# Score masks of three-branch attention: mask products on the TensorE against index selections on the GpSimd

## The reference

```
def _attn(q, k, v, mask=None):
    s = jnp.einsum('bhqd,bhkd->bhqk', q, k) / np.float32(np.sqrt(HD))
    if mask is not None:
        s = jnp.where(mask, s, jnp.float32(-1000000000.0))
    return jnp.einsum('bhqk,bhkd->bhqd', jax.nn.softmax(s, -1), v)
causal = ii[:, None] >= ii[None, :]
o1 = _attn(q, k1, v1, causal[None, None])
o2 = _attn(q, ks, vs)                       # 128 selected keys, no mask
winmask = causal & (ii[:, None] - ii[None, :] < WINDOW)     # WINDOW = 32
o3 = _attn(q, kw, vw, winmask[None, None])
o = g[:, 0] * o1 + g[:, 1] * o2 + g[:, 2] * o3
```

## Time and profile before

| | |
|---|---|
| median of 3 runs | 1062.2 us (1062.18 to 1073.87) |
| profiled execution | 1067.6 us, span 1065.8 us |
| TensorE busy | 909.1 us, 85% |
| VectorE busy | 598.2 us, 56% |
| ScalarE busy | 432.7 us, 41% |
| GpSimd busy | 205.0 us, 19% |

### The profile page before, as it was taken

How to read it: one execution, slowest core, us unless ns; L and a number is a source line. 1 busy time by engine, 2 the same in 40 slices (tenths; PEclk the granted TensorE clock), 3 DMA queues, 4 the chain that set the end, 5 groups by cost and what they waited for, 6 DMA issues and landing times.

```text
span 1065.8 us, 21748 instructions
## 1 busy us (share of the span) xinstructions
PE 909.1 (85%) x8956; PEld 618.8 (58%) x8956; DVE 598.2 (56%) x1687; ACT 432.7 (41%) x724; POOL 205.0 (19%) x274
## 2 busy tenths in 40 slices
PE   3647689999998999989998999899989899888688
PEld 3426456566666666666666666666656565555356
DVE  5243454664587457745874587457755653633433
ACT  0001234452454255425542554255455444436631
POOL 1011100210124012311231123112312320131201
PEclk8658689999999999999999999999999999979855
DMA  7000000100000000000100010000100001200000
GB/s 184 1 1 5 1 6 2 42 21 26 21 21 21 26 21 22 21 26 10 32 21 26 9 33 22 21 6 27 31 21 22 21 26 36 54 21 22 1 4 18
DMA packets 27138, 25.28 MB, mean 24 GB/s; under 512 B 16480, under 2 KB 22240, under 8 KB 26912
## 3 DMA queue, kind: packets, MB, share of 16 engines
q1 hardware_dynamic: 27040, 23.90, 8.0%
HBM read 19.16 MB, written 4.72 MB: 22 GB/s over the span
## 4 chain that ended last, share of the span: by engine, by line
PE 62%; DVE 19%; ACT 8%; issue 6%; DMA 3%; POOL 2%; SPq 1%; DVEq 0%; POOLq 0%; ACTq 0%
PE ring L872 8%; PE side_a L606 5%; PE pv L911 4%; PE pv L893 4%; ACT pr L1114 3%; PE ring L827 3%; DVE rden L1588 3%; PE heads L815 3%; PE side_a L613 2%; PE heads L852 2%; DVE img L1306 2%; PE heads L812 2%; PE side_a L644 2%; PE ring L867 1%; PE ring L835 1%
## 5 line engine op out<-in xcount | busy, mean ns | idle before, releaser
L1114 ACT ACTIVATE pr<-ring 128x1024 f32<-128x1024 f32 (+1 forms) x128 | 120.7, 943 | 116.7 <-PE ring L876 66.1
L872 PE MATMUL ring<-kq 64*128 64x256 f32 (+2 forms) x1280 | 137.9, 343 | 0.8 <-ACT kq L1159 0.5
L872 PEld LDWEIGHTS ring<-kq 64*128 64x128 f32 x1280 | 93.2, 189 | 45.0 <-issue 35.8
L1151 ACT ACTIVATE kq<-ring 128x896 f32<-128x896 f32 x64 | 58.8, 919 | 93.9 <-PE ring L827 93.9
L1573 DVE TENSOR_REDUCE toks<-heads 128x2 f32<-128x512 f32 x64 | 44.2, 691 | 90.2 <-PE heads L857 89.1
L1598 DVE SCALAR_TENSOR_TENSOR ob<-pv,all_gates,scale 128x256 f32<-128x256 f32 x96 | 46.3, 483 | 75.0 <-issue 32.7
L1588 DVE RECIPROCAL rden<-pv 128x256 f32<-128x256 f32 x32 | 56.1, 1754 | 39.7 <-PE pv L893 39.7
L1578 DVE TENSOR_REDUCE toks<-heads 128x4 f32<-128x512 f32 x64 | 44.2, 690 | 53.4 <-PE heads L852 53.1
L606 PE MATMUL side_a<-img,wc_kv 128*128 128x256 f32 x208 | 58.5, 448 | 17.8 <-DVE keep L1309 16.3
L827 PE MATMUL ring<-early,toks 128*128 128x128 f32 x448 | 63.0, 282 | 11.5 <-ACT pr L1114 10.8
L1159 ACT ACTIVATE kq<-ring 128x256 f32<-128x256 f32 x64 | 24.4, 381 | 119.1 <-PE ring L835 119.1
(11 more groups left out here) (372 smaller groups left out, 1761.5 us busy)
## 6 DMA issues: line engine op xcount, KB each, us to landing
scale<-branch_scale SPq DMA_DIRECT2D x128, 96.0 KB, 2.3
branch_scale<-rden SPq DMA_DIRECT2D x32, 128.0 KB, 1.7
late<-in_late SPq DMA_DIRECT2D x1, 2158.5 KB, 8.6
xin<-in_x SPq DMA_DIRECT2D x16, 64.0 KB, 2.2
pr<-in_prep SPq DMA_DIRECT2D x1, 602.0 KB, 4.2
y<-ob SPq DMA_DIRECT2D x8, 64.0 KB, 1.9
kq<-in_masks SPq DMA_DIRECT2D x1, 480.0 KB, 8.6
toks<-in_final SPq DMA_DIRECT2D x1, 434.0 KB, 4.4
```

The source lines that it names most:

```text
L872: m = pe.matmul(ring[:, j, at:at + nq], kq[rows, k, key0:key0 + P], kq[rows, k, Q + q_:Q + q_ + nq], start=r % 2 == 0, stop=at > P)
L1114: act.activation(out, in_, ACT.Exp, scale=SCALE).then_inc(S("exp_done"), 1)
L1151: act.activation(kq[:, k, :], flat[:, 0:WIDE], ACT.Copy).then_inc(S("turned"), 1)
```

## The change

TensorE no longer multiplies masks into the scores; every score product starts and ends its own sum. GpSimd gets a function `scored`, run in part turned (behind the front's and back's slot late and ahead of weighed). It waits for `exp_done` of the step and then overwrites exponentials with zero where an index rule fails, by `affine_select` in place: one instruction of 2 x 128 elements in an even step; four in an odd step (512, 320, 256 and 320 elements), where the third waits for the first and the fourth for the second through the semaphore `later`. The last raises `masked`, and `denominators` waits for `masked` and no longer for `exp_done`.

```
+            def scored(t):
+                for n, r in each(scores_of, t):
+                    k = r // 2
+                    part = pr[:, k // 2 % 2, k % 2, 0:1024] if r % 2 == 0 else pr[:, k // 2 % 2, k % 2, 1024:1856]
+                    part = part.rearrange("p (j n) -> p j n", j=2)
+                    keys = 2 * P + BAND
+                    pool.wait_ge(S("exp_done"), n * PARTS + r + 1)
+                    if r % 2 == 0:
+                        nc.gpsimd.affine_select(part[:, :, 0:P], part[:, :, 0:P], [[0, 2], [1, P]], ALU.is_ge, 0.0, base=0,
+                                                channel_multiplier=-1).then_inc(S("masked"), 1)
+                        continue
+                    own, near = part[:, :, 0:2 * P].rearrange("p j (x n) -> p j x n", x=2), part[:, :, 2 * P:keys]
+                    nc.gpsimd.affine_select(own, own, [[0, 2], [0, 2], [1, P]], ALU.is_ge, 0.0, base=0,
+                                            channel_multiplier=-1).then_inc(S("later"), 1)
+                    nc.gpsimd.affine_select(near, near, [[0, 2], [1, BAND]], ALU.is_ge, 0.0, base=0,
+                                            channel_multiplier=-1).then_inc(S("later"), 1)
+                    pool.wait_ge(S("later"), n * PARTS + r)
+                    nc.gpsimd.affine_select(own[:, :, 1, :], own[:, :, 1, :], [[0, 2], [-1, P]], ALU.is_ge, 0.0,
+                                            base=WINDOW - 1, channel_multiplier=1)
+                    pool.wait_ge(S("later"), n * PARTS + r + 1)
+                    nc.gpsimd.affine_select(near, near, [[0, 2], [-1, BAND]], ALU.is_ge, 0.0, base=WINDOW - 1,
+                                            channel_multiplier=1).then_inc(S("masked"), 1)
...
             run("POOL", [front(n + 1) for n in range(B)], [back(n + 1, n) for n in range(B)],
-                weighed=weighed, filled=filled)
+                turned=scored, weighed=weighed, filled=filled)
...
                 else:
-                    for j in range(2):
-                        pe.matmul(ring[:, j, 0:2 * P + BAND], identb, score_b, start=True, stop=False)
                     pieces = [(0, K1 + P, P, P), (P, KW + P, P, P), (2 * P, KW, 0, BAND)]
...
-                                      kq[rows, k, Q + q_:Q + q_ + nq], start=r % 2 == 0, stop=at > P)
-                if r % 2 == 0:
-                    for j in range(2):
-                        m = pe.matmul(ring[:, j, 0:P], identb, score_b[:, 0:P], start=False, stop=True)
+                                      kq[rows, k, Q + q_:Q + q_ + nq], start=True, stop=True)
...
-                pe.wait_ge(S("exp_done"), of * PARTS + 4 * (g + 1))
+                pe.wait_ge(S("masked"), of * PARTS + 4 * (g + 1))
```

## The result

The changed kernel takes 1105.0 us (median of 4 runs, 1103.7 to 1106.5) against 1062.2 (4 runs, 1058.0 to 1073.9): 1.044 times as long, 95% interval 1.038 to 1.050. The forecast was 1072 in a range of 1044 to 1100. The profiled execution took 1104.0 us, with a span of 1102.3 against 1065.8; the two profiles thus differ by 36.5 us and the medians by 43.

A forecast was written before the change was run, and what follows sets the result against it. TensorE was taken to set the pace in most places. Removal -20, group 2 stall +17, last image +6, group 1 +3, VectorE beside GpSimd +6, closing gaps -2 give +10 on 1062.2: 1072 us, range 1044 to 1100.

The forecast's parts named there:

- The removal, -20 us: Mask products leaving TensorE's chain: gain 20 us, 25 at most, 15 if VectorE takes over more.
- The selections, 3.0 us a pair: GpSimd's price for a pair of heads, even plus odd step, midway between memset (2.0) and two-input rows (4.1).
- The stall of group 2, 17 us: TensorE waits at group 2's denominators for selections queued behind GpSimd's power: 2.8 us in each of images 1 to 6.
- 8 late: Last image: denominators start near 941 us, 8 us late behind the power; 6 us (4 to 8) taken as new.
- Group 1: Denominators of group 1 wait for the selections of step 7: 0.5 us kept, 6 times, 3 us (0 to 8).
- rival C: GpSimd behind the power decides and the clock falls: 1090 us, or 1102 with 2 us for each stall; chance 0.22.
- behind a stall those gaps close: TensorE idles 9% between 550 and 850 us; these gaps shrink behind a stall, so 2 us are taken off.
- VectorE beside GpSimd, 6 us: Some 80 SBUF-only VectorE instructions on the chain wait by chance for selections: 6 us (3 to 11).
- the two lines that I named: VectorE's L1306 and L1463, SBUF-only instructions: both were to have a higher mean.
- A: Cheap selections at the memset's price: 1057 us; chance 0.20.
- B: Stalls are absorbed and the removal's gain is whole, 25 us: 1037 us; chance 0.11.
- D: GpSimd becomes the bound, from 9 us for a pair's selections: 1150 us and more; chance 0.05.

The follow-up runs named there:

- held clock: Three kernels with useless TensorE products and the power in two halves: mask products 1051.9 us, no score masks 1033.7, selections on GpSimd 1050.8.
- the addition alone: Kernel before, mask products kept, plus GpSimd's selections with the denominators waiting for them: 1102.6 us, ratio 1.037.
- the removal alone: Kernel before without the mask products and with no selections, score masks left out altogether: 1054.0 us, ratio 0.988.
- the queue in another order: Changed kernel with selections of steps 10 and 11 earlier in GpSimd's queue and the power cut into two of 16 elements: 1076.1 us, ratio 1.013.
- the idle products: 22 and 40 unused TensorE products ahead of those waiting for `vtok` and `keep`; added to the changed kernel with reordered GpSimd queue: 1044.4 us, ratio 0.987.
- the short power: Changed kernel with the 32-element power on GpSimd replaced by a product of the same size, normalization left out: 1077.1 us, ratio 1.016.
- the change with idle products: Changed kernel, queue order unaltered, plus 22 and 40 unused TensorE products ahead of those waiting for `vtok` and `keep`: 1084.3 us, ratio 1.021.
- no masks and the divided power: Kernel before without score masks or selections, with unused TensorE products and the power in two halves: 1033.7 us, ratio 0.973.
- products and the divided power: Kernel before, mask products kept, with unused TensorE products and the power in two halves: 1051.9 us, ratio 0.988.

## Why the prediction was wrong

**The removal, -20 us.** At a held clock it is 17 us, so the working from the chain was sound. In the kernel alone it is 12 us, and beside the selections nothing. The gain has a condition that the working did not state: the clock must hold.

**The selections, 3.0 us a pair.** They cost 2.39. The middle between memset and two-input rows was too high, the stall depended little on it, and 346 us of GpSimd are under the forecast 400.

**The stall of group 2, 17 us.** It is where I put it, with GpSimd as its releaser: 2.31 us five times, in images 1 to 5, against 2.8 each six times; image 6 has none, and image 0, which I had left out, has 1.33. Together 13 us. With the measured selections the same sum gives 544.52 + 0.41 + 1.01 + 1.99 = 547.9, 2.1 us behind 545.8. The last image cost 7.4 us of waiting against 8 late, and the image took 84.1 us for 77.1 from its first to its last exponential, part of which is the variation of that place told above. Group 1, for which I had 3 us, waits 0.15 us at most.

**The clock, no term at all.** This is the step that failed. I gave the lower clock to rival C alone, at 2 us for each stall, and put it behind the stall. In the sum I took the opposite line: "behind a stall those gaps close", -2 us. In fact the change lengthens gaps at places where VectorE sets the time. The wait for `vtok` grows by the removal (0.93 us before and in the addition alone, 1.28 in the removal alone, 1.29 in the change), the one for `keep` by both parts (2.44 before, 2.90 in the removal alone, 2.71 in the addition alone, 3.19 in the change). Behind these two gaps the clock falls to its lower level, and that costs 4.2 us an image, some 21 us over images 1 to 5, of which the kernel before already lost 7.6 (540.9 against 533.3 us for five images of 106.65 us). The difference, 13.6 us, is the largest part of the 22.0 that the change costs in these images. Part of this hangs on the stall: without the stall and with the gaps as they are (the queue in another order) the idle products are worth 14.3 us in these images. That idle time of TensorE is needed for the loss is shown, since filling the two gaps ends it there. What decides in which image it comes is not: behind the same wait of 1.28 or 1.29 us interval 0 took 4.93 us with the short power, 4.93 or 6.49 in the removal alone, and 6.4 in the change. TensorE's busy time shows it: 30 to 40 us less was expected, 2 came. A row for it stood in the profile before: the convolution's 26 products in 7.59 us in image 3, behind a wait of 2.44, in a stretch whose clock of 0.99 I read as full.

**VectorE beside GpSimd, 6 us.** The term was of the right kind and too small. I spread it by chance over some 80 instructions, which gives 0.75 us an image. The selections' own cost, which holds this term, is 1.8 us an image, 0.7 of it in one place, where a moved instruction of GpSimd lands on VectorE's path each time. By the rule of the Trainium skill (SBUF — State Buffer, Who interferes with whom) a `tensor_scalar` of VectorE from SBUF to SBUF can enter a two-port mode and then excludes an instruction of GpSimd. The trace agrees with an exclusion: 1.70 us alone, 2.60 beside two additions of GpSimd; no row shows the mode. Of the two lines that I named, L1306 has a higher mean as forecast (436 to 565 ns), while L1463, now L1482, ran as before (median 292 ns, longest 696).

**Sum.** Over images 1 to 5 the change costs 22.0 us. The terms give 5 x (-2.52 + 1.83 + 2.38 + 4.24) = 29.6, less the 7.6 that the kernel before loses to its own clock: 22.0. Outside these images the profile shows 14.4 us more: 7.0 in the last image, where 7.4 us of waiting stand behind the power, 6.0 in the tail behind it, 1.4 elsewhere. These I did not take apart. In the tail the granted clock is 0.68 after and 0.73 before, but both places vary by as much between profiles (the last image by 7 us in one kernel). Of the rivals, C was nearest with 1102, by luck: its price of a selection, 4.1 us a pair, was not met (2.39), and its 12 us for the clock belong behind the stall, where the 48 products take 1.79 us in the change as before; only the addition alone and the change with idle products showed them at the lower clock. A and B are ruled out by the stall, D by 31% of GpSimd.

## What to carry to other kernels

Work taken from an engine is worth its time only if the engine then isn't sooner at a place where another sets the pace; in this kernel the time came back as idle time of TensorE, and with it the clock fell and took the rest of the gain. So before a product is removed, look in the timeline for each wait behind it and for whether the same group of products behind it takes longer in one image than in another. In an engine that works in order, put a new step ahead of the longest instruction of its neighbourhood, and check on whose path the steps land that it pushes back.

## What the runs showed that I had not expected

Products without any use make the kernel faster. 62 of them an image take 2.6 us of TensorE, and with the new order of the queue images 1 to 5 take 531.0 us with them against 545.4 without.

The last 35 us run at a mean granted clock of 0.50 or 0.79 in each of the fifteen profiles. The kernel before and the change have 0.50 there. With the new order of GpSimd's queue, or with no masks and the divided power, it was 0.79; with products and the divided power 0.50. TensorE alone, before and then the run with the new order and no idle products:

```profile
1030.00:1065.00 35.00, 30.54 (x172) 0.50 0.07 16
```

```profile
1027.00:1062.00 35.00, 27.21 (x242) 0.79 0.07 16
```

In the same length there are 172 instructions against 242, and the part behind the last exponential takes 116.7 us before and 102.0 in the other, 15 us less. It may differ between executions of one kernel too, though no two profiles of one kernel show it: the products at a held clock spread from 1045 to 1069 us, their profile had 0.50 and was the longest, with a mean clock of 0.92 for the whole execution against 0.93 to 0.94 in the others. What decides which of the two an execution gets was not found. It is also why the medians of whole runs tell less here than the intervals between the exponentials.
